# An attention layer in fp32: VectorE adds the second unit's probabilities to the first's, and the iteration is written out in another order

## The reference

```python
qkv = hidden_states @ Wqkv
scores = jnp.einsum('bqhd,bkd->bhqk', q, k) * scale
scores = jnp.where(causal[None, None], scores + alibi[None], NEG_INF)
probs = jax.nn.softmax(scores, axis=-1)
attn = jnp.einsum('bhqk,bkd->bqhd', probs, v).reshape(B, S, H)
return attn @ Wo
...
x = _layernorm(x + attention(x)); x = _layernorm(x + x @ w_q.T + bias)
```

## Time and profile before

| | us |
|---|---|
| median of 3 runs | 2347.76 |
| the profiled execution | 2347.64 |
| its span, first to last instruction | 2345.9 |
| TensorE busy | 2267.1 (97%) |
| VectorE busy | 1606.7 (68%) |
| ScalarE busy | 996.6 (42%) |
| GpSimd busy | 906.3 (39%) |
| TensorE's granted clock, mean | 0.978 of full |

### The profile page before, as it was taken

The page is one execution under the profiler, slowest core; times in us unless marked ns, Lnnn a source line. Parts: engine busy times, 40 slices in busy tenths (PEclk is TensorE's granted clock), DMA queues, the critical chain, the costliest instruction groups (busy, mean ns, idle before and its releaser), DMA issues. The chain is left out here.

```text
span 2345.9 us, 37013 instructions
## 1 busy us (share of the span) xinstructions
PE 2267.1 (97%) x12600; PEld 1538.3 (66%) x12600; DVE 1606.7 (68%) x4666; ACT 996.6 (42%) x1944; POOL 906.3 (39%) x559
## 2 busy tenths in 40 slices
PE   7999999869999999999999999997999999999997
PEld 5788888645555555555555555535888888888886
DVE  5777777657777877787878787843655555565564
ACT  3222222137777777777777777771111101011010
POOL 0000000007777777777878787870010101101010
PEclk9999999959999999999999999998999999999999
DMA  6454445474333233323332333237232333323320
GB/s 225 157 175 172 169 174 184 148 160 160 92 88 75 70 92 87 81 64 92 88 85 61 91 87 92 53 118 203 81 107 81 97 94 85 98 83 105 94 67 27
DMA packets 176819, 255.97 MB, mean 109 GB/s; under 512 B 15118, under 2 KB 104846, under 8 KB 176162
## 3 DMA queue, kind: packets, MB, share of 16 engines
q1 hardware_dynamic: 176176, 253.69, 37.3%
q10 hardware_dynamic: 498, 0.49, 0.1%
HBM read 166.04 MB, written 87.03 MB: 108 GB/s over the span
## 5 line engine op out<-in xcount | busy, mean ns | idle before, releaser
L1008 DVE CUSTOM_DVE_ANT_0 unused<-pa,distance 128x512 bf16<-128x512 f32 (+3 forms) x1536 | 772.5, 554 | 238.1 <-PE pa L845 212.8
L986 ACT ACTIVATE probs<-pa,slope 128x512 f32<-128x512 f32 (+3 forms) x1536 | 765.6, 592 | 259.9 <-PE pa L868 119.8
L823 POOL TENSOR_TENSOR probs<-probs 128x1024 f32<-128x1024 f32 x252 | 673.5, 2673 | 86.3 <-ACT probs L986 63.4
L845 PE MATMUL pa<-k,ff_hi 96*128 96x512 f32 (+1 forms) x1008 | 319.4, 374 | 23.6 <-DMA ff_hi<-q_lo_d 20.2
L1237 POOL TENSOR_TENSOR yb<-y,bias 128x1024 f32<-128x1024 f32 x32 | 76.6, 2394 | 655.4 <-DVE z L1260 631.0
L882 PE MATMUL pa<-probs,v 128*32 128x512 f32 (+3 forms) x3072 | 300.7, 494 | 1.2 <-issue 0.8
L868 PE MATMUL pa<-ff_hi,k 116*128 116x512 f32 (+1 forms) x798 | 300.0, 415 | 0.1
L845 PEld LDWEIGHTS pa<-k,ff_hi 96*128 96x128 f32 x1008 | 185.8, 193 | 142.5 <-DVE mx L1008 86.6
L809 POOL TENSOR_SCALAR_AFFINE_SELECT probs<-probs 128x512 f32<-128x512 f32 x256 | 158.7, 637 | 192.9 <-ACT probs L986 192.9
L1201 ACT ACTIVATE ln<-ln 128x1 f32<-128x1 f32 x64 | 13.0, 203 | 498.2 <-DVE ln L1280 498.2
L302 PE MATMUL ps<-xt_hi,wq_hi 128*128 128x512 f32 (+1 forms) x552 | 220.7, 400 | 2.8 <-DVE k_lo L511 2.8
(11 more groups left out here) (120 smaller groups left out, 3018.2 us busy)
## 6 DMA issues: line engine op xcount, KB each, us to landing
ff_hi<-q_hi_d SPq DMA_DIRECT2D x84, 256.0 KB, 5.6
x_in<-in_L_attn_hidden_states SPq DMA_DIRECT2D x8, 2048.0 KB, 9.1
q_hi_d<-q_hi SPq DMA_DIRECT2D x64, 256.0 KB, 2.0
q_lo_d<-q_lo SPq DMA_DIRECT2D x64, 256.0 KB, 2.4
att_d<-att SPq DMA_DIRECT2D x64, 256.0 KB
x_in<-in_L_attn_hidden_states SPq DMA_DIRECT2D x32, 512.0 KB, 3.8
out<-z SPq DMA_DIRECT2D x32, 512.0 KB, 2.6
k<-k_d SPq DMA_DIRECT2D x32, 384.0 KB, 7.9
```

The costliest lines, as they stand in the source:

```text
L823: nc.gpsimd.tensor_tensor(o, o, probs[:, source % PR, h0:h1, 0:N], ALU.add).then_inc(add_done, 1)
L845: nc.tensor.matmul(bank[:, 0:keys], q3[u][0:3 * D, qb // BPH, h, qb % BPH * P:(qb % BPH + 1) * P], k3[u][0:3 * D, k0:k0 + keys], start=Tru ...
L986: nc.scalar.activation(probs[:, n % PR, h, 0:N], sc_ps[sc_ring.bank[use]][:, at:at + N], ACT.Exp, scale=slope[:, bass.ds(g * HPG + h, 1)]) ...
L1008: nc.vector.tensor_tensor_reduce(out=unused[:, use % MXB, 0:keys], in0=bank[:, 0:keys], in1=distance[:, d0:d0 + keys], scale=1.0, scalar=- ...
```

## The change

There are four edits.

1. A VectorE instruction in each iteration, `add_second`, adds unit 1's probabilities (into which GpSimd has added 2 and 3) to the last 384 columns of unit 0's, for all four heads. It stands at step 5 behind that step's evacuation, waits for V0, V1 and GpSimd's two adds, and counts `vector_added`. The ones product of unit 0 then gives the sums of the whole half; O1 is gone from `plan`.
2. O0 waits for `vector_added`, and ScalarE waits for it before it writes over unit 1's buffer.
3. `plan` is written in another order: an iteration begins with a maximum and V7 of the iteration before; V6 stands in step 8 of its own iteration; V4, V5 and O0 stand together in step 6 behind T. `pool_order` cuts 2 before 0, and adds 7 into 8 ahead of the cuts of 10 and 11. The evacuation of half 0 is at step 5 instead of 4.
4. TensorE's wait for the maxima's rows stands at the step's first S instead of at its start.

```diff
@@ -579,31 +579,33 @@
 
 
     plan = [
-        "V6- S M M M S S M S L V7- M M M",
-        "S S S M M V9- V10- M S M M",
-        "S M O8- V11- M M S",
-        "S M",
-        "S M M O9- V0 V1 S M S M M S V2 V3 O0 M",
-        "S M M S S M S V4 M M",
-        "S S M S M M S M",
-        "S M O1 M S M S M S M",
-        "S M S M M S M S M",
-        "S V5 S M T M S M S",
-        "S M O4 S",
-        "S M M M V8",
+        "M V7- M S M S M M V9- M S M M S L O8- M M",
+        "S S M S M M V10- S M M",
+        "S S M M",
+        "S M V11- O9- M M",
+        "S S M V0 V1 M S M M S",
+        "S M S M V2 V3 S S",
+        "S M M T V4 V5 O0 M S M S M S M M",
+        "S M S S M M S M",
+        "S S M M S M S M V6",
+        "S M M S S M M S O4 V8 M",
+        "S S",
+        "S M M",
     ]
     plan = [step.split() for step in plan]
     assert sum(step.count("M") for step in plan) == len(pieces)
 
     pool_order = [
-        ("cut", 0), ("cut", 1), ("cut", 2), ("cut", 3),
+        ("cut", 2), ("cut", 0), ("cut", 1), ("cut", 3),
         ("add", 2, 1, 0, 4), ("add", 3, 1, 0, 4), ("add", 5, 4, 0, 4), ("add", 6, 4, 0, 4),
-        ("cut", 9), ("cut", 8), ("cut", 10), ("cut", 11),
-        ("add", 7, 8, 0, 2), ("add", 7, 8, 2, 4), ("add", 11, 9, 0, 4), ("add", 10, 9, 0, 4),
+        ("cut", 8), ("cut", 9), ("add", 7, 8, 2, 4), ("add", 7, 8, 0, 2),
+        ("cut", 11), ("add", 11, 9, 0, 4), ("cut", 10), ("add", 10, 9, 0, 4),
     ]
 
-    evacuate_at = {2: (1, 1), 4: (0, 0)}
+    evacuate_at = {2: (1, 1), 5: (0, 0)}
     sums_at = {2: (1, 1), 8: (0, 0)}
+
+    add_at = 5
     cuts = [x[1] for x in pool_order if x[0] == "cut"]
     CUTS = len(cuts)
     TAIL = ["V%d" % n for n in range(NU) if any("V%d-" % n in step for step in plan)] + ["O%d" % n for n in range(7, NU)]
@@ -703,6 +705,7 @@
         mxt_hi_done = sem("mxt_hi_done")
         exp_done, cut_done = sem("exp_done"), sem("cut_done")
         pv_done, att_done, sums_done, add_done = sem("pv_done"), sem("att_done"), sem("sums_done"), sem("add_done")
+        vector_added = sem("vector_added")
         sums_back, recip_done = sem("sums_back"), sem("recip_done")
         att_stored = [sem(f"att_stored{c}") for c in range(HALF)]
         block = ctx.enter_context(nc.Block())
@@ -888,7 +891,9 @@
                 c, kb = units[n]
                 lo, N = span(units[n])
                 mine = [x[1] for x in block_list if x[0] == "O" and units[x[1]][0] == c and x[2] == t]
-                if (t, n) in added_to:
+                if n == 0:
+                    pe.wait_ge(vector_added, t + 1)
+                elif (t, n) in added_to:
                     pe.wait_ge(add_done, added_to[t, n])
                 elif n in cuts:
                     pe.wait_ge(cut_done, t * CUTS + cuts.index(n) + 1)
@@ -928,10 +933,10 @@
                     pe.wait_ge(loaded[nu], (i + (2 if nu == 0 else 1)) * LOADS)
                 for n in range(NU):
                     maxima, products, j = maxima_of(t, n), blocks_of(t, n), 0
-                    if n in (0, BPH):
-                        pe.wait_ge(neg_max[u][n // BPH], (i + 1) * PUTS)
                     for kind in plan[n]:
                         if kind == "S":
+                            if j == 0 and n in (0, BPH):
+                                pe.wait_ge(neg_max[u][n // BPH], (i + 1) * PUTS)
                             scores(t, u, n, j)
                             j += 1
                         elif kind[0] in "VO":
@@ -976,6 +981,8 @@
                     if old >= 0:
                         ot, on = old // NU, old % NU
                         act.wait_ge(pv_done, max(block_done.get((kind, on, ot), 0) for kind in "VO"))
+                        if on == 1:
+                            act.wait_ge(vector_added, ot + 1)
                         if (ot, on) in read_by_add:
                             act.wait_ge(add_done, read_by_add[ot, on])
                     for h in range(HPG):
@@ -1021,6 +1028,14 @@
                 nc.vector.scalar_tensor_tensor(out=mxt_lo[:, m, :], in0=src, scalar=-1.0, in1=raw(mxt_hi[:, m, :]),
                                                op0=ALU.mult, op1=ALU.subtract).then_inc(mx_free, 1)
 
+            def add_second(t):
+
+                dve.wait_ge(pv_done, max(block_done["V", n, t] for n in (0, 1)))
+                dve.wait_ge(add_done, added_to[t, 1])
+                N, at = span(units[1])[1], span(units[1])[0] - span(units[0])[0]
+                o = probs[:, 0, :, at:at + N]
+                nc.vector.tensor_tensor(o, o, probs[:, 1 % PR, :, 0:N], ALU.add).then_inc(vector_added, 1)
+
             def evacuate(t, c):
 
                 dve.wait_ge(pv_done, block_done["V", (BPH - 1, NU - 1)[c], t])
@@ -1037,6 +1052,8 @@
                         reduce_item(w, item)
                     if n in evacuate_at and t >= evacuate_at[n][0]:
                         evacuate(t - evacuate_at[n][0], evacuate_at[n][1])
+                    if n == add_at:
+                        add_second(t)
                     if last and n == BPH:
                         dve.wait_ge(sums_back, 16)
                         nc.vector.reciprocal(early[:, :], early[:, :]).then_inc(recip_done, 1)
```

## The result

The changed kernel takes 2403.75 us (median of 4 runs, 2400.84 to 2405.45) against 2347.41 for the kernel before (4 runs, 2346.43 to 2350.14): 1.0236 times as long, 95% interval 1.0222 to 1.0251. Forecast were 2322 us, between 2304 and 2350. The profiled execution of the changed kernel took 2400.84 us with a span of 2399.0, so 53.1 us more than the span before; its mean granted clock was 0.969, where it had been 0.978.

A forecast was written before the change was run, and what follows sets the result against it. The prediction took TensorE as the bound, with other engines close behind and VectorE full in one stretch. From 2347.6 us, 40 off over 31 periods and 14 back in the last iteration gave 2322 us, range 2304 to 2350.

The forecast's parts named there:

- maxima of units are as many as before: VectorE's maxima in the attention stage: their number does not change, so this was listed among cost-free edits.
- the cuts move within GpSimd's queue: GpSimd's reordered cuts: listed as cost-free, since its queue has idle time behind ScalarE before most of them.
- GpSimd's add goes first: Rival: GpSimd's add holds the inputs, VectorE's new add waits 4.61 us; 3.3 us more an iteration, 2464 us; chance 0.04.
- The last iteration: Attention stage's end: evacuation and add stand behind the reciprocal, which waits for a DMA; 14 us lost, between 9 and 18.
- The period: One steady iteration of the attention stage: 32.0 us against 33.3, so 1.3 us less; gain bounds 0.45 and 1.7.
- part 1: Iteration from the start of V6 to the end of V1, in the old order: 13.2 us before, 13.0 forecast.
- part 2: Iteration from the end of V1 to the start of O4: 16.9 us before, 15.4 forecast from two near limits.
- part 3: Rest of the iteration, from the start of O4: 3.2 us before, 3.4 forecast with one score product more.
- hardly late: O0 waiting for the new add in part 2: TensorE's other work covers 5.7 us of the chain's 5.8.
- O1's 0.78 us: Unit 1's ones product on TensorE, removed: 0.8 of the 1.3 us gained an iteration, 24 us at most over 31.
- VectorE's add lies on the path whole: Rival: the full stretch is longer by 1.76 us and shorter by 0.78; 44 us more in all, 2392; chance 0.11.
- only O1's time is gained: Rival: the new chain eats the order's gain; 24 us gained, 14 back, 2338 us; chance 0.15.

The follow-up runs named there:

- by form: The changed kernel with the small two-column maximum written as a reduction of one input instead of two: 2346.97 us, ratio 1.0005 to the kernel before.
- by place: The changed kernel with GpSimd's cut of unit 11 between its two adds of unit 7 into 8 and the reciprocal late, two-input maximum kept: 2338.99 us.
- late reciprocal: The changed kernel with the last iteration's reciprocal behind the evacuation of half 0 and the add; alone, two-input maximum kept: 2411.06 us, ratio 1.0293.
- the kernel with both remedies: The changed kernel with the one-input maximum and the last iteration's reciprocal behind evacuation and add: 2331.98 us, ratio 0.9946; in five later rounds 2330.62 us.
- the new order without the add and the remedies: The changed kernel without VectorE's add and with O1 back, two-input maximum and early reciprocal kept: 2439.74 us, ratio 1.0412.
- the kernel before with the cut moved: The kernel before with GpSimd's cut of unit 11 moved behind its two adds of unit 7 into 8: 2363.14 us, ratio 1.0073.

## Why the prediction was wrong

- **The step that failed: "maxima of units are as many as before" and "the cuts move within GpSimd's queue", both under the edits costed at nothing.** The number of maxima is the same, but the neighbour of the small maximum in GpSimd's queue is another one: a cut before, an add now. Its own price went from 0.175 to 2.38 us in 23 of 31 periods, 42 us, and the gaps brought 13 more through the clock. Undone by form (2346.97) or by place (2338.99, with the late reciprocal too), those costs are gone. The prediction asked of the new big add whether GpSimd and VectorE disturb each other and did not ask it of the small old instruction, which took 0.175 us. It called the question open, since no add of VectorE is seen beside a GpSimd add in the trace before. That is true of adds alone: the 31 held layer-norm instructions of the last stage, above, answered it in that same trace.
- **The rival "GpSimd's add goes first" had the mechanism at the wrong instruction.** At the big add it went as the forecast said: GpSimd's add comes second and takes 5.00 us instead of 4.60 (1091.42 and 1096.59, above), 0.4 us where the prediction had counted with up to 0.9.
- **The last iteration**: 17.2 us, forecast 14, between 9 and 18. The chain is as described. The sum came to 12, and 2 were added for the clock. Three terms were short. ScalarE took 14.6 us from unit 6 on and not 12.3 (1620.74 to 1635.3); with the late reciprocal, where the clock was full, it still took 13.5 (1599.97 to 1613.45), so only about half of this is the clock. The 1.0 us taken off at the end for V6 did not come: it is 5.9 us from there to the end of the last copy, as before. And unit 6 started some 1.7 us later than reckoned, counted from the last small maximum (33.9 us, reckoned 32.2); V4 and V5 at half clock are 1.6 of that (3.54 for 1.93), which the 2 us for the clock had foreseen. The forecast took the order of reciprocal and evacuation as given; with the reciprocal behind both, 15.0 us come back (2346.97 to 2331.98), since the DMA's data is there only 9.3 us after the evacuation runs (1595.54 and 1604.80).
- **The period.** Forecast 32.0, bounds 31.6 to 32.85; without the held maxima it is 32.76, just within. By parts, where nothing is held: part 1 took 13.56 for 13.0, part 2 15.89 for 15.4, part 3 3.3 for 3.4. Part 1 took 0.56 us more than the sum; why is not shown, and that VectorE works in it too is only a guess. In part 2, O0 was late by 0.7 us in 29 of 30 iterations, where it had been "hardly late".
- **O1's 0.78 us.** The prediction says that in the full stretch an instruction of TensorE taken away gives nothing by itself. The two windows above speak against it: O1 counted whole. The gain was 0.91 from the exchange and -0.36 from the order, not 0.8 and 0.5.
- **The add beside other work**: 1.76 us as forecast. O0's wait of 0.7 us for it is the part that reached TensorE. The rival "VectorE's add lies on the path whole" gave 2392, near the time that came, and that nearness is chance: the kernel with both remedies has the add and is faster than before.
- **The size of the gain.** Without the two accidents the stage gains 15.1 us in 31 periods. The forecast was 40, bounds 14 to 53, and the rival "only O1's time is gained" 24: even the part that went right lies at the lower bound.

## What to carry to other kernels

When an order is changed, list for each two-input VectorE instruction on SBUF, the small ones too, what GpSimd does at that moment before and after; an instruction of 16 elements can last as long as GpSimd's. The cheap cure is a form with one input, and it costs 0.01 us. A first look costs one line per instruction: where the longest is far above the shortest (219/220/858 ns in the kernel before, 174/2378/2383 in the changed one), something holds it at times, and the timeline of GpSimd beside it says whether that is an add. In an in-order queue, an instruction that waits for a DMA goes behind everything that others wait for.

## What the hardware showed that I had not expected

- A few ns in start decide between 0.17 and 2.38 us. In the three kernels with such a tie and the two-input form, all 62 held maxima had the add ahead by 6 to 17 ns, and the others by at most 6. Two of these kernels spread from 2381.7 to 2420.6 and from 2421.08 to 2448.73 us, where those without held maxima, or with one held every time, spread by 2 to 9. The changed kernel itself, with the tie, spread by only 4.6. Much of the spread goes with the granted clock of the runs (0.975 to 0.960 in the first, 0.970 to 0.963 in the second).
- A reduction with one input beside the same GpSimd add, started into it, took 0.19 us in all 31 iterations that had the add there.
- A gap of 1.5 us on TensorE in an otherwise full stretch was followed by 3.4 to 6.8 us at half clock in 7 of 23 cases, and in 16 by nothing. In the kernel with the late reciprocal alone it was 7 of 21, in the new order without the add and the remedies 11 of 17. In the kernel before with the cut moved, the gaps were 0.6 us and none was followed by it.
